# Decoder layer, one core: first layer norm's transposed rows made by GpSimd from group 4 on, early constants moved behind the first layer norm, instruction orders set anew

## What is computed

```
def _layernorm(x): m, v = mean(x), var(x); return (x - m) / sqrt(v + 1e-5)
# linear attention: q = elu(x Wq.T + bq) + 1, k = elu(x Wk.T + bk) + 1, v = x Wv.T + bv
#   out = sum_{t<=s} (q_s . k_t) v_t / (sum_{t<=s} q_s . k_t + 1e-6);  return out @ Wo.T + bo
# cross attention: softmax(q k.T / 4) v, q from x, k and v from ctx_1024 (128 tokens)
# ffn: h = silu(x W1.T * s1) * (x W2.T * s2); h = gelu(h H1.T * s); h = gelu(h H2.T * s); return h W3.T * s3
x = x + linear_attention(_layernorm(x))
x = x + cross_attention(_layernorm(x), ctx_1024)
x = x + ffn(_layernorm(x))
```

## Time and profile before

| | |
|---|---|
| median of 3 runs | 1068.17 us (1066.75 to 1068.72) |
| time of the profiled execution | 1067.3 us |
| its span, first to last instruction | 1065.5 us |
| PE busy | 1041.3 us, 98% |
| DVE busy | 769.4 us, 72% |
| ACT busy | 527.6 us, 50% |
| POOL busy | 262.1 us, 25% |
| granted TensorE clock | 1.00 of full speed over the run |

### The profile page before, as it was taken

How to read it: one execution, slowest core, us unless ns; L and a number is a source line. 1 busy time by engine, 2 the same in 40 slices (tenths; PEclk the granted TensorE clock), 3 DMA queues, 4 the chain that set the end, 5 groups by cost and what they waited for, 6 DMA issues and landing times.

```text
span 1065.5 us, 25693 instructions
## 1 busy us (share of the span) xinstructions
PE 1041.3 (98%) x10186; PEld 866.9 (81%) x10186; DVE 769.4 (72%) x1708; ACT 527.6 (50%) x855; POOL 262.1 (25%) x363
## 2 busy tenths in 40 slices
PE   7999999999999999999999999999999999999998
PEld 7989877878877888778788878787888888787886
DVE  5999998767996879867798778987678455523412
ACT  4344553855536635556454556374633635433432
POOL 3323352100441114301161111620026001500600
PEclk9999999999999999999999999999999999999999
DMA  4687766443643444534645334453364435544552
GB/s 161 230 296 244 260 225 209 159 133 105 214 149 125 139 154 144 165 124 135 192 150 169 118 107 156 157 156 115 129 209 157 144 119 199 172 146 158 180 177 80
DMA packets 76742, 174.87 MB, mean 164 GB/s; under 512 B 10960, under 2 KB 26448, under 8 KB 76624
## 3 DMA queue, kind: packets, MB, share of 16 engines
q1 hardware_dynamic: 73168, 161.70, 45.1%
q10 hardware_dynamic: 3456, 11.54, 3.8%
HBM read 145.38 MB, written 39.35 MB: 173 GB/s over the span
## 4 chain that ended last, share of the span: by engine, by line
PE 84%; DVE 10%; issue 2%; DMA 2%; POOL 0%; ACT 0%; SPq 0%; ACTq 0%; DVEq 0%; POOLq 0%
PE bank L1254 43%; PE bank L1141 8%; PE bank L1239 6%; PE bank L1274 6%; PE bank L1113 5%; PE bank L1082 5%; PE bank L1097 3%; PE bank L1087 2%; DVE hidden_full L1020 2%; PE bank L1058 2%; DVE mx L989 2%; DVE hidden_full L1023 1%; PE bank L1191 1%; PE bank L1134 1%; PE bank L1122 1%
## 5 line engine op out<-in xcount | busy, mean ns | idle before, releaser
L1254 PE MATMUL bank<-hidden_a,weight_ring 128*128 128x512 f32 x1024 | 251.3, 396 | 0.0
L1254 PE MATMUL bank<-hidden_b,weight_ring 128*128 128x512 f32 x1024 | 248.1, 395 | 0.3 <-DVE inexact_flag L1045 0.3
L1254 PEld LDWEIGHTS bank<-hidden_b,weight_ring 128*128 128x128 f32 x1024 | 187.8, 188 | 39.4 <-issue 0.8
L1254 PEld LDWEIGHTS bank<-hidden_a,weight_ring 128*128 128x128 f32 x1024 | 187.2, 188 | 40.0 <-issue 1.4
L857 ACT ACTIVATE hidden_full<-bank,columns_sb 128x512 f32<-128x512 f32 x128 | 88.2, 689 | 221.8 <-PE bank L1254 221.3
L706 POOL TENSOR_TENSOR ve<-mv,eps 128x1 f32<-128x1 f32 (+1 forms) x80 | 21.1, 264 | 474.5 <-DVE mv L872 474.5
L1239 PE MATMUL bank<-hidden_b,weight_ring 128*128 128x512 f32 x512 | 123.0, 394 | 1.4 <-DMA weight_ring<-weights_scratch 1.4
L745 POOL TENSOR_TENSOR hidden_a<-hidden_full,hidden_a 128x512 fp32r<-128x512 f32 x64 | 83.0, 1297 | 167.9 <-ACT hidden_a L852 166.7
L1239 PEld LDWEIGHTS bank<-hidden_b,weight_ring 128*128 128x128 f32 x512 | 94.2, 188 | 21.3 <-DMA weight_ring<-weights_scratch 1.8
L1028 DVE TENSOR_TENSOR hidden_a<-hidden_full,hidden_a 128x512 fp32r<-128x512 f32 x64 | 43.6, 683 | 70.8 <-ACT hidden_a L863 70.6
L989 DVE TENSOR_REDUCE mx<-bank 128x4 f32<-128x512 f32 x128 | 80.3, 678 | 16.6 <-PE bank L1141 16.3
(11 more groups left out here) (135 smaller groups left out, 1696.4 us busy)
## 6 DMA issues: line engine op xcount, KB each, us to landing
weight_ring<-weights_scratch SPq DMA_DIRECT2D x160, 512.0 KB, 3.5
weights_scratch<-in_h ACTq DMA_DIRECT2D x16, 512.0 KB, 5.0
xn3T_scratch<-hidden_b SPq DMA_DIRECT2D x16, 512.0 KB, 4.0
weight_bits<-in_h SPq DMA_DIRECT2D x32, 256.0 KB, 3.6
weight_ring<-weights_scratch SPq DMA_DIRECT2D x32, 256.0 KB, 2.8
values_scratch<-hidden_full SPq DMA_DIRECT2D x14, 512.0 KB, 4.6
xv<-values_scratch SPq DMA_DIRECT2D x14, 512.0 KB, 4.2
x_in<-in_x SPq DMA_DIRECT2D x16, 256.0 KB, 2.8
```

Of the source, the lines that this page charges most:

```text
L1254: mm = eng.matmul(pbank(step, g, n)[:, :], ring[:, slot, kk * P:(kk + 1) * P], src[:, part, kk, :], start=(kk == 0 and part == 0), stop=(k ...
```

## The change

From group 4 on (`REMADE = 4`) the turned rows of the first layer norm are no longer made by PE. x is also given to the kernel in a turned copy `xT`, made on the host as `ctxT` is. For each of the 12 groups:

- DVE still makes the mean and variance from `x_in`, but not `ln1`. POOL writes 1/sqrt to `stats1_out` and copies the mean beside it.
- Four new DMAs are issued by SP: `load_xT` (256 KB, over `x_in`, when the statistics are made), `keep_stats1` (2 KB to DRAM), and `load_stats1` twice (256 values read as a row of all 128 partitions, 128 KB; first the means, then 1/sqrt, into one buffer, so that the second waits for POOL to have used the first).
- POOL subtracts the mean (`xn1` 0, two instructions of 128x256) and multiplies (`xn1` 1, two more).
- The four transposes are gone. ACT (L764 before) and DVE (L879 before) read `x_t`, which is `x_in`, in place of the PSUM bank. The next `load_x` waits for DVE's `ln1T`.

At the start: the table load of ACT stands ahead of the wait for `cst`. The columns are issued behind two weights. DVE's three small vectors stand behind the first `ln1`, ACT's one ahead of the first `q`. `FILL` goes from 24 + 20 + 40 + 20 matmuls to 22 + 14 + 24. All `LEAD` and `OFFSET` values, `PATIENCE`, and the assumed times of `split`, `copy_weights` and `load_bits` are new, and so the lists of all engines.

```diff
+    REMADE = 4
-    SPARE, PATIENCE, HOLD, MANY = 1, 14.5, 0, 3
+    SPARE, PATIENCE, HOLD, MANY = 1, 17.2, 0, 3
...
-    LEAD = {("gpsimd", "bias"): 18.2, ("gpsimd", "ctx"): -146.3, ("gpsimd", "gate_rest"): -222.4,
+    LEAD = {("gpsimd", "bias"): 282.9, ("gpsimd", "ctx"): -679.5, ("gpsimd", "gate_rest"): -407.6,
...
+        if g < REMADE:
+            steady("ln1", vector=-12.6, took=dict(vector=.75))
+            steady("ln1T", tensor=-10.5, scalar=-8.63, vector=-7.75, took=dict(tensor=.4, scalar=.52, vector=.6))
+        else:
+            steady("load_xT", sync=-30, took=dict(sync=5))
+            steady("keep_stats1", sync=-25, took=dict(sync=2.2))
+            for n in range(2):
+                steady("load_stats1", n, sync=-24 + 4 * n, took=dict(sync=3))
+                steady("xn1", n, gpsimd=-20 + 4 * n, took=dict(gpsimd=1.75))
+            steady("ln1T", scalar=-8.63, vector=-7.75, took=dict(scalar=.52, vector=.6))
...
+                    elif step == "load_xT":
+                        eng.wait_ge(LN1["mean_var"], GB * g + GB)
+                        eng.dma_start(x_t, xT.rearrange("(c p) t -> p c t", p=P)[:, :, T * g:T * g + T]).then_inc(xT_loaded, 16)
+                    elif step == "keep_stats1":
+                        eng.wait_ge(LN1["rstd"], g + 1)
+                        eng.wait_ge(mean1_copied, g - REMADE + 1)
+                        eng.dma_start(st1_d[g].rearrange("w p b -> p w b"), stats1_out[:, :, :]).then_inc(stats1_stored, 16)
+                    elif step == "load_stats1":
+                        eng.wait_ge(stats1_stored, 16 * (g - REMADE + 1))
+                        if n == 1:
+                            eng.wait_ge(xn1_centred, g - REMADE + 1)
+                        elif g > REMADE:
+                            eng.wait_ge(xn1_made, g - REMADE)
+                        eng.dma_start(stats1[:, :, :].rearrange("p s b -> p (s b)"),
+                                      st1_d[g, n].rearrange("s b -> (s b)").partition_broadcast(P)).then_inc(stats1_loaded, 16)
...
+                    elif step == "xn1":
+                        half = x_t.rearrange("p c (b s) -> p c b s", b=GB)
+                        mean_or_rstd = stats1[:, :, :].rearrange("p s b -> p b s")
+                        if n == 0:
+                            eng.wait_ge(xT_loaded, 16 * (g - REMADE + 1))
+                        eng.wait_ge(stats1_loaded, 32 * (g - REMADE) + 16 + 16 * n)
+                        for c in range(C):
+                            last = eng.tensor_tensor(half[:, c], half[:, c], mean_or_rstd, (ALU.subtract, ALU.mult)[n])
+                        last.then_inc((xn1_centred, xn1_made)[n], 1)
...
-                FILL = {("ln1T", 0, 0): 24, ("q", 0, 0): 20, ("xv", 0, 0): 40, ("lin_scores", 0, 1): 20}
+                FILL = {("ln1T", 0, 0): 22, ("q", 0, 0): 14, ("lin_scores", 0, 0): 24}
```

More of the change, by code:

```diff
@@ L201, in needs @@
                     + ([d("keep_v", KEPT[-1])] if g == 0 else [])
-            return {"ln1T": [t(step, g), t("v", g - 1)], "split": [], "ctx": [d("load_ctx", g), t("xk", g - 1), t("xv", g - 1)],
+            return {"ln1T": [t(step, g) if g < REMADE else p("xn1", g, 1), t("v", g - 1)], "split": [], "ctx": [d("load_ctx", g), t("xk", g - 1), t("xv", g - 1)],
                     "q": [t(step, g), v("k_heads", g - 1)], "k": [t(step, g), v("q", g)], "xq": [t(step, g), t("x_scores", g - 1, 1)],
@@ L211, in needs @@
         if engine == "vector":
[L212 removed]
+            return {"ln1_stats": [d("load_x", g), d("keep_stats1", g - 1)], "ln1": [p("ln1_stats", g)], "split": [a(step, g)], "ln1T": [a(step, g)],
                     "q": [a(step, g), t("lin_scores", g - 1, 1)], "k": [a(step, g)], "k_heads": [v("k", g), t("lin_scores", g - 1, 1)],
@@ L701, in _, with ln_rstd @@
                 eng.wait_ge(ln_const, 2)
-                def ln_rstd(ln, which, b0, n, count, done):
+                def ln_rstd(ln, which, b0, n, count, done, out=rstd):
                     eng.wait_ge(ln["mean_var"], count)
@@ L708, in ln_rstd @@
                     eng.wait_ge(ln["ve"], done)
-                    eng.tensor_tensor(rstd[:, which, b0:b0 + n], ve[:, which, b0:b0 + n], mhalf[:, 0:1].broadcast_to([P, n]), ALU.pow)\
+                    eng.tensor_tensor(out[:, which, b0:b0 + n], ve[:, which, b0:b0 + n], mhalf[:, 0:1].broadcast_to([P, n]), ALU.pow)\
                        .then_inc(ln["rstd"], 1)
@@ L761, in _ @@
                     if step == "ln1T":
-                        eng.wait_ge(xn1_turned, g + 1)
-                        wait_count(eng, v_psum, g)
-                        eng.activation(xn1T[:, 0, :, :], halves(pbank(step, g)), ACT.Copy).then_inc(xn1T_hi, 1)
+                        if g < REMADE:
+                            eng.wait_ge(xn1_turned, g + 1)
+                            wait_count(eng, v_psum, g)
+                        else:
+                            eng.wait_ge(xn1_made, g - REMADE + 1)
+                            eng.wait_ge(v_psum, g)
+                        eng.activation(xn1T[:, 0, :, :], halves(pbank(step, g)) if g < REMADE else x_t, ACT.Copy).then_inc(xn1T_hi, 1)
                     elif step == "split":
@@ L868, in mean_var @@
                 def mean_var(ln, which, src, g, b):
+                    if which == 0 and b == 0 and g > REMADE:
+                        eng.wait_ge(stats1_stored, 16 * (g - REMADE))
                     eng.bn_stats(stats[:, which, b, :], src).then_inc(ln["stats"], 1)
@@ L937, in _ @@
                         eng.wait_ge(xn1T_hi, g + 1)
-                        rest(xn1T, pbank(step, g)[:, :]).then_inc(xn1T_done, 1)
+                        rest(xn1T, pbank(step, g)[:, :] if g < REMADE else x_t.rearrange("p c t -> p (c t)")).then_inc(xn1T_done, 1)
                     elif step == "ln2T":
```

106 lines of the change are left out of this document (62 added, 44 removed).

## The result

The changed kernel takes 1075.0 us in the median of 7 runs (1072.95 to 1080.65), the kernel before 1068.17 (7 runs, 1065.46 to 1069.16) beside it. The ratio is 1.0076, 95% interval 1.0051 to 1.0100: 8 us slower, where 12 us less were forecast, outside the range and on the wrong side. The profiled execution took 1073.23 us. Four disturbed executions of 1426 to 5518 us (two of the kernel before, one each of e12 and e16) count in no ratio.

What follows compares the result with a forecast made beforehand. The prediction took PE's own work, busy 1041.3 of 1065.5 us, plus its few waits as the bound. From 1067.3 us, 5.2, 2.4, 2.0 and 2.7 off and 1.0 added gave 1056.0, stated as 1056.5 us; range 1050 to 1065.

Steps and rivals of the forecast that it cites:

- Terms 1 and 2: PE's list: twelve turns gone, 5.2 us; 24 fewer changes between kinds of work or array shapes, 2.4 us.
- term 3: Kernel start: statistics and first q earlier, PE's list ahead at the second linear scores; 2.0 us (0 to 3).
- term 2: PE's list: 24 fewer changes between kinds of work or array shapes; 2.4 us (0 to 3).
- Term 4: PE's waits for keys at the max line: four fewer of about 0.9 us each; 2.7 us (0 to 4).
- Term 5: DVE beside POOL's new rows: 14.5 us of DVE work gone, about 7 us of holding by POOL; booked 0.
- Term 6: PE's waits: some places late under the new orders that were not before; 1.0 us added (0 to 5).
- third rival: SP's queue: the longer statistics chain delays key loads and max; slower, 1080 at 2 us a group; chance 0.05.

Runs made afterwards that it cites:

- e12: Changed kernel with SP's store and loads of statistics kept, but POOL reads a tile of ones and doesn't wait for the loads; 1068.71 us, ratio 1.0020.
- e16: Changed kernel with the moves of e15, and POOL's subtraction of group 5 moved behind the context rows of group 13; 1086.82 us, ratio 1.0177.
- experiment 2: Changed kernel, same lists, without the statistics' store and loads through DRAM; POOL uses a tile of ones; 1064.29 us, ratio 0.9976 to the kernel before.
- experiment 3: Kernel before, own lists, PE's four transposes of the first layer norm made one one-column matmul from group 4 on; 1066.28 us, ratio 0.9991.
- experiment 4: Kernel before with its own lists and fills, only the code of the start changed; 1068.10 us, ratio 0.9999.
- experiment 6: Changed kernel without the statistics' trip, as in experiment 2, and POOL's 48 new pieces cut to 128x8 elements; 1064.83 us, ratio 0.9973.
- e17: Changed kernel, group 9's rows moved: ACT's part behind two gelus, DVE's behind the rest of the first; 1076.59 us, ratio 1.0087.
- e18: Changed kernel run again as it is, nothing edited; 1073.88 us, ratio 1.0078 to the kernel before.
- e15: Changed kernel, group 9's rows moved: ACT's part behind four gelus, DVE's part behind the division of group 5; 1080.72 us, ratio 1.0140.
- e8: By the order of the runs the same as experiment 6: changed kernel without the statistics' trip, POOL's new pieces cut small; 1064.83 us, ratio 0.9973.

## Why the prediction was wrong

**Terms 1 and 2, what leaves PE's list: right in kind, small in part, and not paid out.** With the median step of each kind in the trace of before laid along both lists of PE, the list has 1026.7 us before and 1018.3 now, 8.4 less (an estimate). That is not the 7.6 of the two terms come true: about 3 us of it are the 44 fills fewer (part of term 3), twelve turns at 0.354 are 4.3, and what is left for term 2 is about 1 us, not 2.4. The transposes of `x_in` are 16, as forecast, but PE's busy time fell by 3.0, not 5 to 8; steps at a clock of 0.50 count in it at their full length, and without the trip (experiment 2, 1036.2 us) it fell by 5.1. In experiment 3, 3 us taken off PE under the order of before gave 1.0 us (at most 2.6): over half is given back at other steps, with DVE's and ACT's work unchanged. I priced a turn with no cover. The whole turn, 0.35 and 0.02 behind it, was not tried, so what it would have given stays open. Term 2 alone was not tried either.

**Term 3, the start: the lead was there and was spent.** DVE's statistics started at 3.65 and `q` at 9.41, both as forecast, 1.9 us ahead. The second linear scores came at 27.48, 0.6 us ahead and not 2, though fewer fills stand before them. The step that failed is that the lead lasts. Two waits of PE take it:

```profile
13.88 1.29 POOL L789 TENSOR_TENSOR xb<-xb,bob 128x512 f32<-128x512 f32 x1 [2.14 <-DMA bob<-in_bo]
```

```profile
17.49 0.66 PE L1117 MATMUL bank<-cst,x_in 128*128 128x128 f32 x4 [1.65 <-DVE x_in L931]
...
22.44 1.17 PE L1200 MATMUL bank<-qf,kz 32*128 32x128 f32 x32 [1.52 <-issue]
```

POOL's power for the first layer norm of group 1 stands behind its bias rows, which waited for `bob`, and DVE's rows and PE's turn of group 1 wait for the power. The exponential of `k` came at 16.66 us, as forecast (16.7), but the first linear scores need DVE's `kz` too, which stands in DVE's list behind `v` and the rest of group 1's rows and ended at 22.33; the scores, at 20.67 before, start at 22.44. What the whole start was worth no run shows: experiment 4 had the old fills, and so no lead.

**Term 4, waits for keys: mis-sized.** L1200 still waits 4.7 us at four places (longest 2.3) where L1141 waited 5.3 at six: 0.6, not 2.7.

**Term 5, the new POOL rows beside DVE: right that they cost no time.** 48 pieces of 0.782 us (0.94 forecast), POOL 300.0 us busy (305 forecast), and their work costs nothing that was measured (experiment 6). DVE's busy time fell by 3.4, not 7. The holding itself is there, and at one place it costs: the two instructions for `nshift`, 0.17 and 0.18 us in e17 near 350 us, took 0.82 and 0.77 beside POOL's residual rows:

```profile
571.26 0.82 DVE L1057 TENSOR_SCALAR nshift<-mx 128x16 bf16<-128x16 f32 x1
572.12 0.77 DVE L1059 SCALAR_TENSOR_TENSOR nshift<-mx,nshift 128x16 bf16<-128x16 f32 x1
```

```profile
571.15 3.48 POOL L779 TENSOR_TENSOR residual<-residual,stats 128x256 f32<-128x256 f32 x4
```

PE waited 2.20 us for the second, and 1.56 in experiment 2, where the pair took 0.82 and 0.77 too. So some 1.2 us of it are the holding, by rows of the third layer norm that the change left as they were; it comes from how the new lists fall together here, and not from the trip or the new rows. The Trainium skill (GPSIMD Engine Reference, Key points) says that GpSimd contends with VectorE instructions in a two-port mode or with two SBUF inputs. That such instructions are held agrees with these rows; whether only these kinds are, they don't tell.

**Term 6, new waits: the step that failed.** I booked +1.0 us (up to 5). By the prediction's own count, PE idle less the start's wait less 3.5 at the end, 15.2 us before are now 33.1 - 4.4 - 3.5 = 25.2: +10.0. Steps at the lower clock come on top: all that the span holds beyond PE's list as priced above was 1065.5 - 1026.7 = 38.8 us and is 1071.4 - 1018.3 = 53.1, so +14.3 against 8.4 saved. These are two single executions. By the ratios the kernel lost 8.1 us where its list is 8.4 shorter, 16.5 in all; of that 10.7 is the trip (experiment 2), and 5.8 are the new lists' own (below).

The nearest I came is the third rival, which I gave 0.05. That the trip holds SP's queue was right, but its path and its point of decision were not. It saw `max` delayed by keys; those waits did not grow (term 4), and the queue with its traffic cost 4.7 us by another way, (b) below. The larger part, 6 us by subtraction, came with POOL's wait, which the rival did not name. And it was to decide at 1 us a group; measured were 10.7/12 = 0.9, and that was enough to make the kernel slower because the rest of the change gave 2.6 us and not 12. The argument that I set against it, that key loads stand ahead of the waiting rows, looked at one neighbour of one queue. It missed (a) that the load back then stands behind the keys, 5.97 us, and POOL behind that with context rows that PE needs; (b) that `weight_bits` stands behind the store in SP's queue, with DVE's list behind it; (c) the price of the store; (d) the clock. I took (c), 3.4 us, from the third layer norm's store in the earlier trace rows. The new one is slower in the same run (DMA view of e18: count, KB each, median us to landing):

```profile
stats_scratch<-mv SPq DMA_DIRECT2D x16, 2.0 KB, 3.5
stats_scratch<-stats_out SPq DMA_DIRECT2D x12, 2.0 KB, 5.9
```

Both move 2 KB. In the kernel's code the old one writes a partition's four values in one row of DRAM and the new one in two rows of two; whether that is the reason no run tests. The trip's price was 9.3 us for each group with nothing hidden in my own working, 112 us in all, and I took less than a hundredth of it as the likely value.

Even without the trip the change gave 2.6 us where 8.4 left PE's list. In the windows view (columns as in the earlier trace rows) of before, of the changed kernel and of experiment 2, PE's busy time from 86 to 142 us is:

```profile
86.00:142.00 56.00, 54.23 (x745) 48.94 (x744) 52.54 (x128) 27.11 (x53) 17.27 (x26) 1.00 0.79 254
```

```profile
86.00:142.00 56.00, 48.42 (x715) 45.12 (x715) 47.95 (x116) 23.34 (x47) 22.88 (x36) 0.97 0.74 224
```

```profile
86.00:142.00 56.00, 50.23 (x763) 47.05 (x759) 50.52 (x123) 23.75 (x48) 24.47 (x38) 0.97 0.70 221
```

In that phase, where DVE is nearly full, the new list leaves PE idle 4 to 6 us more with the trip or without. Why the list fits worse there was not settled: it would take the change of one step at a time, each with its own plan. Also open is how the 6 us of POOL's wait divide between its own list (context rows, powers) and ACT's.

## What to carry to other kernels

A round trip through DRAM that replaces a local step must be priced with everything that stands behind its waits on each in-order list, the queue's own included: follow SP, POOL, ACT and DVE one by one, and ask of each what the next step is and who needs it. Work that leaves the busiest engine is worth its price only where the engines that feed it have time left; drop it alone, under the old order, before believing the sum (here 1.0 us, where about 3 us of steps were taken out). And check that the step put in its place is free: here it kept 0.13 of 0.35 us. An idle row names what was waited for, not what the time would be without it: of three edits of places made by such rows (e15 to e17), none made the kernel faster. A fill must stand in the wait that it is to cover, ahead of the very step that waits.

## What the runs showed of the hardware

The new store of 2 KB took 5.67, 5.89, 6.07 and 6.10 us from issue to landing at the four places followed in the turns (changed kernel, e12, e18), and 5.9 us in the median of e18, against 3.5 for the third layer norm's store of 2 KB in the same run. The loads of 128 KB at these places took from 3.2 to 6.2 us. One wait of PE of 3.4 us was followed by 5 us at a granted clock of 0.50, which nearly doubled its price; one of 2.2 us left the clock at 1.00. Times of one kernel spread by several us whatever it holds: 1071.5 to 1081.0 us for the changed kernel (e18), 1061.0 to 1069.0 without the trip (e8), 1065.1 to 1070.8 for the kernel before beside it.
